# Second layer: where on GpSimd the broadcast of a tile's expert weights is issued, and the order of the last front tiles

## What is computed

```python
y, g = jnp.split(xf @ shared_gw.T, 2, axis=-1)
shared = jax.nn.silu(g) * y @ shared_dw.T
scores = jax.nn.sigmoid(xf @ gate_w.T)
_, topk_idx = jax.lax.top_k(scores + gate_bias, 2)
w = jnp.take_along_axis(scores, topk_idx, axis=-1)
w = w / jnp.sum(w, axis=-1, keepdims=True)
for e in range(8):
    we = jnp.sum(jnp.where(topk_idx == e, w, 0.0), axis=-1)
    g_e, u_e = jnp.split(xf @ up_w[e].T, 2, axis=-1)
    out = out + (jax.nn.silu(g_e) * u_e) @ down_w[e].T * we[:, None]
...
x = x + attention(layernorm(x)) * silu(shared + out)
```

## Time and profile before

| what | us |
|---|---|
| median of 3 runs | 2076.19 (2070.89 to 2077.12) |
| profiled execution, time | 2082.67 |
| its span, first to last instruction | 2080.9 |
| TensorE busy in it | 1955.8 (94%) |
| VectorE | 1406.1 (68%) |
| ScalarE | 880.2 (42%) |
| GpSimd | 683.5 (33%) |

### The profile page before, as it was taken

The page is one execution under the profiler, slowest core; times in us unless marked ns, Lnnn a source line. Parts: engine busy times, 40 slices in busy tenths (PEclk is TensorE's granted clock), DMA queues, the critical chain, the costliest instruction groups (busy, mean ns, idle before and its releaser), DMA issues.

```text
span 2080.9 us, 33061 instructions
## 1 busy us (share of the span) xinstructions
PE 1955.8 (94%) x11618; PEld 1434.5 (69%) x11618; DVE 1406.1 (68%) x3474; ACT 880.2 (42%) x1753; POOL 683.5 (33%) x846
## 2 busy tenths in 40 slices
PE   5889999999999999999999999999999989999998
PEld 3566676766767667686676766767677766767666
DVE  6847758477575775757766676666766567675773
ACT  3534624345252452515524264243543436333462
POOL 2633413243142441414414143133332334232341
PEclk8999999999999999999999999999999999999999
DMA  8647332262322524234242442415332163421630
GB/s 265 213 144 245 100 101 61 72 208 83 102 77 97 172 73 118 71 128 147 63 112 81 161 128 64 106 63 185 118 89 68 62 200 115 103 61 42 204 101 16
DMA packets 105261, 240.46 MB, mean 116 GB/s; under 512 B 16700, under 2 KB 26940, under 8 KB 104840
## 3 DMA queue, kind: packets, MB, share of 16 engines
q1 hardware_dynamic: 85080, 173.44, 27.8%
q0 software_dynamic: 14256, 43.94, 6.8%
q10 hardware_dynamic: 5760, 20.97, 3.0%
HBM read 179.67 MB, written 57.82 MB: 114 GB/s over the span
## 4 chain that ended last, share of the span: by engine, by line
PE 75%; DVE 12%; DMA 5%; issue 3%; ACT 1%; POOL 1%; DVEq 0%; ACTq 0%; POOLq 0%; SPq 0%
PE bank L452 22%; PE bank L616 15%; PE bank L535 11%; PE bank L501 11%; PE bank L551 8%; DVE bank L794 4%; DMA qring<-mneg 4%; PE bank L637 3%; DVE nmax L797 3%; PE bank L508 2%; PE bank L561 2%; PE bank L514 1%; DVE probs L812 1%; PE bank L463 1%; DVE xn L746 1%
## 5 line engine op out<-in xcount | busy, mean ns | idle before, releaser
L452 PE MATMUL bank<-xnT,upring 128*128 128x512 f32 (+1 forms) x2208 | 713.5, 405 | 1.4 <-DVE hbuf L837 1.4
L794 DVE CUSTOM_DVE_ANT_0 bank<-bank,mask_strip 128x512 f32<-128x512 f32 (+1 forms) x768 | 479.0, 635 | 197.6 <-PE bank L501 195.6
L696 ACT ACTIVATE probs<-bank 128x512 f32<-128x512 f32 (+1 forms) x720 | 388.2, 555 | 282.8 <-PE bank L535 256.6
L452 PEld LDWEIGHTS bank<-xnT,upring 128*128 128x128 f32 x2208 | 405.4, 194 | 60.4 <-DVE hbuf L837 9.2
L501 PE MATMUL bank<-kring,qring 127*128 127x128 f32 (+3 forms) x1280 | 379.5, 350 | 23.0 <-DVE nmax L794 14.7
L535 PE MATMUL bank<-qring,kring 128*128 128x512 f32 (+1 forms) x880 | 358.2, 411 | 40.8 <-DMA qring<-mneg 19.3
L616 PE MATMUL bank<-wdown,hbuf 128*128 128x256 f32 x1408 | 324.4, 380 | 0.0
L501 PEld LDWEIGHTS bank<-kring,qring 127*128 127x128 f32 x1280 | 227.1, 193 | 114.5 <-DVE nmax L794 62.6
L616 PEld LDWEIGHTS bank<-wdown,hbuf 128*128 128x128 f32 x1408 | 263.4, 190 | 35.5 <-issue 1.7
L535 PEld LDWEIGHTS bank<-qring,kring 128*128 128x128 f32 x880 | 169.1, 194 | 128.8 <-issue 44.9
L1662 POOL TENSOR_SCALAR_AFFINE_SELECT probs<-probs 128x512 f32<-128x512 f32 x200 | 128.3, 642 | 369.1 <-ACT probs L696 368.7
(11 more groups left out here) (165 smaller groups left out, 2309.4 us busy)
## 6 DMA issues: line engine op xcount, KB each, us to landing
upring<-up_img SPq DMA_DIRECT2D x136, 512.0 KB, 4.0
upring<-up_img ACTq DMA_DIRECT2D x40, 512.0 KB, 5.6
q_img<-probs SPq DMA_DIRECT2D x32, 512.0 KB, 3.3
kring<-k_img SPq DMA_DIRECT2D x64, 256.0 KB, 3.0
qring<-q_img SPq DMA_DIRECT2D x32, 384.0 KB, 4.7
qring<-q_img SPq DMA_DIRECT2D x192, 64.0 KB, 2.0
q_img<-probs SPq DMA_DIRECT2D x32, 256.0 KB, 4.0
k_img<-probs SPq DMA_DIRECT2D x16, 512.0 KB, 5.7
```

The lines of the kernel that those rows point to most:

```text
L452: last = nc.tensor.matmul(out_ap, part_a(a, pa, k), part_b(b, pb, k), start=(n == 0), stop=(n == len(steps) - 1))
L696: nc.scalar.activation(pr, pr if biased else scores, ACT.Exp, scale=scale).then_inc(s_exp, 1)
L794: nc.vector.tensor_tensor_reduce(scores, scores, mask_strip[:, T - w:T], 1.0, -BIG, ALU.add, ALU.max, nmax[:, u % 2, g0, qt:qt + 1]).then_ ...
```

## The change

In every unit of the second layer the load of the tile's weights becomes the first thing that GpSimd does, ahead of the masks: `gate_load(TILE_AFTER[u])`. So the load of tile j is issued at the start of the unit to which tile j belongs, one unit later than before (for tile 14 in unit 4: ahead of the first mask and not behind it). In unit 11 it stands behind the layer norm's factors. The multiply stays behind the first mask. In unit 4 the multiply of tile 12 comes ahead of the first mask, that of tile 13 behind it; before they stood behind the first and the second mask.

```diff
@@ pool_batch, for u in range(UNITS[0], U_ALL)
                         for half in (0, 1):
                             pool_norm(pool, 0, half)
+                    if u == UNITS[0]:
+                        weigh(pool, FRONT_TILES[-2])
+                    gate_load(pool, TILE_AFTER[u])
                     for kt in range(NT):
...
-                        if u == UNITS[0] and kt < 2:
-                            weigh(pool, FRONT_TILES[kt - 2])
-                            gate_load(pool, FRONT_TILES[kt - 2] + 2)
-                        if u > UNITS[0] and kt == 0:
-                            weigh(pool, TILE_AFTER[u - 1])
-                            gate_load(pool, TILE_AFTER[u - 1] + 2)
+                        if kt == 0:
+                            weigh(pool, FRONT_TILES[-1] if u == UNITS[0] else TILE_AFTER[u - 1])
```

## The result

The changed kernel takes 2116.41 us (median of 4 runs, 2114.25 to 2117.94) against 2075.19 (2070.89 to 2077.12) for the kernel before in the same comparison: a ratio of 1.0203, 95% interval 1.019 to 1.0217. It is 41 us slower. The forecast was 2100 with a range of 2076 to 2120: the sign was right and the time lies in the range, but 16 us above the forecast, close to the rival "full delay everywhere" (2123).

The account below looks back on a forecast made before the run. TensorE's first score matmul of a unit was taken to wait for the row, an 8 KB DMA of negated maxima. Terms 30 - 7 + 4 - 3 = +24 us, added to the median 2076.2, gave 2100; range 2076 to 2120.

Parts of the forecast that it names:

- full delay everywhere: Rival: every load and the down weights hold the row in full; +47 us, 2123; chance 0.08 (+38 and over).
- +12 to +38: Band of change in us given to the forecast itself, a mixture at the tied places; chance 0.60.
- The sum from the upper ends, +47: Whole program: loads at their upper bound 41, unit 5 gaining 0, down weights +5.9; +47 us.
- The load 0.57 us ahead of the row: Units 5 to 10: GpSimd issues the moved load some 0.57 us before SyncE issues the row.
- Unit 8, one DMA of 128 partitions: +1.0 a batch: Unit 8's start: the row stands behind a load landing after 3.6 us, so the unit starts 1.0 us later.
- a tie in time, so I take the middle, 30: Load delays at units 6 to 11, 19 to 41 us in all; second DMAs of pairs tie with the row; 30 taken.
- If the row wins, 10.1 us of waits go [...] I take 7: Unit 5's start: with tile 15's load later, gain of at least 0, at most 11.3 us; 7 taken.
- The down weights, +4: First batch, unit 5: the 1.8 MB DMA leaves 0.57 us ahead of the row; 0 to +5.9 us, +4 taken.
- The waits that the row has anyway, -3: Units 6 to 10: some five us of existing row waits no longer count where the load delays more; about -3 us.
- third rival: Unit 4: tile 13's load lands later, TensorE waits for masks; at most +16 on top of the first rival, 2101; no separate chance.
- first rival: Only the first DMA of a pair holds the row, and unit 5's row goes free; +9 us, 2085; chance 0.18.
- faster rival: The load misses the row, no start is delayed, and unit 5 gets 11 us back; 2065; chance 0.08.

Follow-up runs that it names:

- e4: Changed kernel, but in units 5 to 11 the second DMA of a load pair waits until the row has landed; 2096.31 us, ratio 1.0092.
- e1: Changed kernel with the load of a unit's tile moved back behind the unit's first mask and multiply; 2071.87 us, ratio 0.9977.
- e8: Changed kernel, with the first batch's down weights held until the row of unit 5 has landed; 2125.92 us, ratio 1.0224.
- e10: The kernel of e8 run again, on the same chip as e9; 2125.61 us, ratio 1.023.
- e7: The kernel of e2 with the loads of tiles 15 to 21 left out, so multiplies use stale weights; 2066.24 us, ratio 0.994.
- e6: Changed kernel, load first only in units 4 and 5; from unit 6 it goes behind the first mask and multiply; 2086.93 us, ratio 1.0044.
- e5: Changed kernel, load waits for ScalarE's copy of the maxima, which also releases the row; down weights wait for the row; 2070.69 us, ratio 0.9962.
- e3: Changed kernel in the same order, but each load waits until its unit's row has landed, and the down weights wait too; 2069.76 us, ratio 0.9962.
- e9: The changed kernel, unaltered, run again on the same chip as e10 and e11; 2125.67 us, ratio 1.0224.
- e2: The kernel of e1 with the first batch's down weights held until the row of unit 5 has landed; 2068.74 us, ratio 0.9958.
- e11: The kernel of e2 run again, on the same chip as e9 and e10; 2069.04 us, ratio 0.9957.

## Why the prediction was right, and where it was wrong

**The bound was read rightly.** The prediction asked what the change does to the row. The starts and the experiments agree: within their noise the row is the whole effect.

**The number was right by its range, not by its forecast.** Measured +41 is outside the +12 to +38 that had 0.60, and in the part "+38 and over" that had 0.08; the range held it because it reached to 2120. The sum from the upper ends, +47, also leaves out the -3 that the other two sums have. With it, it is +44, and the measurement lies 3 below.

**The load 0.57 us ahead of the row.** Measured 0.59 to 0.60 in nearly every unit 5 to 10. Right.

**Unit 8, one DMA of 128 partitions: +1.0 a batch.** Measured +1.17 (2.47 to 3.64). Right. The sign that was named for it, landings of 3.1 to 3.3 us in every batch, held in five of eight; the others took 3.4, 3.7 and 4.6.

**Units 6, 7, 9 and 10: "a tie in time, so I take the middle, 30". This step failed.** There was no tie. The second part left 0.00 to 0.08 us ahead of the row in each batch, and the landings were 3.0 to 3.3 us in most, which is the upper bound. Against the undisturbed 2.33 us the four pairs cost 33 us, where the upper bound is 32 and the middle 21. Units 6 to 11 gave 38.6 us against before; the prediction had 30 - 3 = 27. e4 prices the second parts of all units at 20 us. The prediction had rows at hand that spoke for this: its own step put the second part ahead of the row (0.03), and the earlier trace rows are a full delay by a second part 0.4 us ahead. To take the middle between two ends meant to assume that half of the rows would win, where the fixed order of instructions gave the same lead each time, to 0.08 us.

**Unit 5: "If the row wins, 10.1 us of waits go [...] I take 7". This failed with it.** Measured, outside the first batch, +0.6. In six batches the load of tile 15 left 0.59 us ahead of the row and its 112 partition part 0.07 ahead (0.9 and 0.4 before the change), and the row was held as before. In the first batch it came behind the down weights. Behind the row it fell only in the sixth (by 0.09 us). That the gain was there to be had is shown by e1: 2.0 us instead of 3.2 to 3.75, once the load is behind the row.

**The down weights, +4.** Right. Measured +3.1 at the start of the first batch's unit 5. The timelines after, with the row's landing (us to landing, minimum, median, maximum), answer to the earlier trace rows:

```profile
185.49 0.58 POOL L1674 DMA_DIRECT2D wdown<-in_w_down  x1
186.07 1.08 POOL L1612 DMA_DIRECT2D gring<-gate_img  x2
...
186.10 0.56 SPq L426 DMA_DIRECT2D qring<-mneg  x1
...
DMA to landing us min/median/max: 6.3/6.3/6.3
...
192.58 0.47 PE L535 MATMUL bank<-qring,kring 128*128 128x512 f32 x1 [4.53 <-DMA qring<-mneg]
```

The row landed after 6.3, not after the 9 that was named as a sign: that was the upper end, where the sum had taken a value between. The row waited for a part of the 1.8 MB only. One cost was not in the sum, the clock behind the wait (1.5 us, last section). By e8 and e10 this term can't be saved alone.

**The waits that the row has anyway, -3.** At the starts of units 6 to 10 such waits make 5.9 us in the kernel before, and they are there in e7 too (9.0 + 1.5 us in all). They were not simply absorbed: of the changed kernel's rows under a load two landed after 4.3 and 4.6 us, each with a packet of instructions in flight. How much was absorbed is left open.

**Unit 4.** The prediction's third rival, TensorE waiting for the masks of unit 4, did not happen; the starts of unit 4 are 1.0 us earlier in sum.

In its own terms the sum is now 38.6 + 0.6 + 3.1 - 1.0 = 41.3, where it had 27 - 7 + 4 = 24. Of the 17 us missing, 12 are the middle of the pairs and 8 unit 5, less some 2 of the rest: both answer one question, what a DMA issued in the same tenth of a microsecond does.

**The rule and the rivals.** The Trainium skill, page "DMA: Bandwidth & Descriptors", section "Queues, rings and completion order", was read so that the row waits for one share of the load at most, since an engine goes round the queues packet by packet. In this trace the row waits for both parts of a pair (e4: 20 us), and the runs decide: the first rival (2085), which rests on this reading, is wrong. They don't show that the engines go round otherwise. At the start shown above the row's 32 packets ran from 1.49 to 2.33 us behind its issue, among those of the load (0.84 to 2.30); it is the reading that a second part counts for nothing that fails. The faster rival (2065) put its point "about 0.1 us behind the row's issue"; it lies somewhat later, at 0.11 to 0.27 (e6, e5). Its time is nearly what e1 to e3 reach (2069 to 2072), and the changed kernel misses it because its load is 0.6 us ahead.

## What to carry to other kernels

If a small DMA gates the bound engine, look for every transfer on any queue that is issued in the microsecond ahead of it, and put it behind, by a wait on the same event if the order of instructions can't do it. Between two ends of an unknown, ask whether the case is one that repeats: here the hand-written order put 38 of 40 second parts within 0.08 us ahead of the row, so one of the ends held and not the middle. Moving a large transfer behind one critical DMA is no gain until you have seen what it delays next.

## What the runs showed of the hardware that was not expected

**A transfer that is issued a little later can still come first.** With a second part on GpSimd's queue 0.00 to 0.08 us ahead of it (and the first 0.6 ahead) the row landed after 2.9 to 3.6 us in most cases, against 1.8 undisturbed. A load 0.09 us behind it had packets ahead of the row's (one case, landing 2.56); 0.11 us behind it, with 16 partitions 0.41 ahead, it was 3.4 (one case). At 0.27 us behind there was no loss: e5 has the ratio of e3, and all but one of its late rows at units 6 to 11 had a packet of instructions in flight, as in e7; that one (4.3 us, first batch) followed the down weights.

**TensorE's clock after a wait.** In the first batch of the changed kernel TensorE stood idle for 4.53 us, and 0.8 us after it had started again its granted clock fell to half. Three stretches behind the wait (columns as above):

```profile
192.40:195.00 2.60, 2.42 (x7) 1.95 (x8) 1.35 (x3) 1.62 (x3) 0.00 (x0) 0.69 0.50 132
195.00:198.00 3.00, 3.00 (x11) 2.31 (x10) 1.96 (x7) 1.77 (x5) 0.79 (x2) 0.70 0.79 272
198.00:204.00 6.00, 5.90 (x38) 4.42 (x42) 5.35 (x14) 3.77 (x8) 4.00 (x6) 1.00 0.01 3
```

The same start in the kernel before, behind a wait of 1.5 us:

```profile
194.20:197.00 2.80, 2.76 (x12) 2.14 (x12) 2.01 (x5) 2.13 (x5) 0.00 (x0) 1.00 0.88 343
```

The clock was at half for 3.4 us in all, and the unit took 1.5 us longer. In e6, with 5.82 us of idle time, it was at half for 6.8 us, the first 3 of them before the idle time had ended, and this unit took 1.7 us longer (the expectation of e8 says 4.7, which is what three such units of e6 make together). In e8 one stretch at half clock followed a wait of 1.8 us in the third batch:

```profile
709.20:713.90 4.70, 4.68 (x14) 3.80 (x15) 2.87 (x7) 2.87 (x5) 0.35 (x1) 0.64 0.28 72
713.90:719.00 5.10, 5.10 (x30) 4.18 (x28) 4.44 (x13) 4.03 (x8) 3.11 (x5) 1.00 0.37 143
```

Such stretches are in every kernel here (13 in the profiled execution of before, 10 after, 17 in e9, the same kernel as after), many of them at like places of successive batches (324.6, 580.6 and 833.1 us in before). So over the whole program the changed kernel doesn't have more of them as a rule. In the second layer's units it does. From its first score matmul to the issue of the next row a unit takes 9.15 to 9.38 us in 704 of the 728 cases (units 4 to 10 of all thirteen traces). The other 24 take 10.6 to 11.4 us, each with a stretch at half clock in it. All 24 follow a wait for the row of 1.77 us or more, and of such waits there are 44; behind the 684 shorter waits, or none, it never happened. The kernel before, e2, e7 and e11 have no such unit, after has 1, e9 4, e10 5 and e8 6. So a longer wait for the row can cost another 1.4 us and more.

These units are a part of why e9 is 9 us slower than the first comparison of the same kernel (1.0224 against 1.0203, overlapping intervals). 3 of the 9 us are in the kernel before on that chip too. The profiled execution of e9 took 17 us longer than that of after: 4.2 in the starts, 5.2 in these units, and the rest elsewhere, with 32 us more at half clock in all. Why its rows came later and its clock fell more often stays open.
